# Softcapped attention: inverse norms are spread, and sums of squares turned, by transposes where products with the identity did it

## The chip, the core and the metric

The kernel runs on one core of a Trainium2 chip. A core has five engines that work side by side and wait for each other by semaphores: TensorE (PE in the profile, its weight loads PEld), VectorE (DVE), ScalarE (ACT), GpSimd (POOL) and SyncE (SP), which issues DMAs. TensorE reads a stationary operand (the weight load) and a moving one from SBUF and writes to PSUM, which has eight banks of 512 float32 a partition. The metric is the time on the device in microseconds, the lower the better.

## The reference

The program is a chain of sixteen layers on 1024 tokens of width 256 (mixers and feed-forward layers in turn), all in float32 but for a few bfloat16 parts. The change touches one layer, an attention of 16 heads of width 128 with normed queries and keys and a soft cap on its scores:

```python
q, k, v = x @ wq.T, x @ wk.T, x @ wv.T          # 16 heads of 128
q = rmsnorm(q, q_norm_w)                        # x * rsqrt(mean(x * x) + 1e-6) * w
k = rmsnorm(k, k_norm_w)
q, k = apply_rope(q, cos, sin), apply_rope(k, cos, sin)
scores = einsum('bhtd,bhsd->bhts', q, k) * 128 ** -0.5
scores = 50.0 * tanh(scores / 50.0)
...                                             # causal mask, softmax, times v, times wo
```

## The kernel before

`capped_attention` works on one head at a time, and makes the next head's operands while it works on this one. q and k lie with the width of the head (128) on the partitions and the 1024 tokens along the row, in two halves of 512. The rotation and the norms' weights enter as one factor for each row (`pair`). What is left of the two norms is one number for each token: the inverse root of its mean square.

The steps of a head, all in the order of one list that TensorE, VectorE and GpSimd follow:

```python
STEPS = "s0 s1 q0 s2 k0 o0 s3 q1 o1 s4 k1 o2 s5 o3 s6 m0 v0 s7 t0 v1 s8 s9 s10 b0 s11 b1 o4 o5 o6 o7".split()
```

The steps s and o belong to this head, the others make the next one. s0 to s3 are the scores of the first 512 queries with key tiles 0 to 3, s4 to s11 those of the second 512 with key tiles 0 to 7 (line 1602; narrower beyond the diagonal, so s8 has 512 columns, s9 384, s10 256, s11 128). ScalarE takes the tanh of each (line 1654) and the exponential of the unit before it (line 1661), in the order tanh 8, exponential 7, tanh 9, exponential 8. GpSimd multiplies the 128 columns on the diagonal by the causal mask (line 1519); for s8 that is mask 4. o0 to o7 (line 1611) are the outputs of the eight query tiles, over t + 1 key tiles each; output t waits for mask t and for a free bank of two. VectorE divides by the sum.

Of the makes, q, k and v are products with the weights (lines 1584 and 1593), copied by VectorE. GpSimd squares q and k. Step m (line 1558) sums the squares over the partitions, by four products with ones that leave each sum on 32 equal rows of a quarter of the bank: 128 rows of 512. VectorE makes means of them (line 1698). Step t (line 1567) turns these, so that tokens lie on the partitions: four products whose stationary operand is a 128x128 piece of `means` and whose moving operand is every 32nd column of the identity, four columns. VectorE copies the 16 columns (line 1703), and GpSimd raises them to the power -0.5 (line 1511): `inverse`, with columns 0 to 7 for the queries and 8 to 15 for the keys. The keys' norm is applied as the scale of the tanh. The queries' must be spread over all rows: step b (line 1590), twice four products with one column of `inverse`, broadcast to 128x128, as the stationary operand and the identity as the moving one. VectorE multiplies q by the result (line 1720), which ends the making of a head; the first score of the next head waits for it.

Head 0 is made ahead of all scores, in the order q0 k0 q1 k1 v0 m0 t0 v1 b0 b1; there ScalarE and VectorE make the inverse root. The last head has no makes beside it.

Of the kernel before, what the change touches and what calls it, by code (L numbers as in the profile page):

```python
# [13 lines left out]
P = 128  # L14
TOK = 1024
D = 256
NT = TOK // P
# [1404 lines left out]
QUARTER = P // 4  # L1422


def capped_attention(core, name, w, turns, heads, softcap):
# [5 lines left out]
    nc, x, hT = core.nc, core.x, core.hT  # L1431
    scale = P ** -0.5 / softcap
    NU = len(UNITS)
    with ExitStack() as layer:
        rows = layer.enter_context(nc.sbuf_tensor(f"{name}_rows", [P, NT, heads * P], F32))
        wo = layer.enter_context(nc.sbuf_tensor(f"{name}_wo", [P, heads, D], F32))
        with Stage(core, name) as st:
# [5 lines left out]
            means = st.sb("means", [P, HALF])  # L1443
# [3 lines left out]
            inverse = [st.sb(f"inverse{n}", [P, 2 * NT]) for n in range(2)]  # L1447
# [10 lines left out]
            ps_out, ps_sums = [core.bank(pairs[2] + n) for n in range(2)], core.bank(pairs[1] + 1)  # L1458
# [24 lines left out]
            @block.sync  # L1483
            def _(sp):
                for h in range(2, heads):
                    sp.wait_ge(made, (h - 1) * NM - 2)
                    sp.dma_start(w[h % 2][:], core.dram[f"{name}_w"][h]).then_inc(w_in[h % 2], 16)
                sp.dma_start(wo[:], core.dram[f"{name}_wo"]).then_inc(wo_in, 16)
                sp.wait_ge(wo_in, 16)
# [56 lines left out]
            @block.tensor  # L1546
            def _(pe):
                pe.sem_inc(summed, TILES)

                def make(h, e, step):  # L1550

                    kind, half = step[0], int(step[1])
                    if kind == "m":
                        if h == 0:
                            pe.wait_ge(filled, 9)
                        pe.wait_ge(squared, h * 4 + 4)
                        for n in range(4):
                            last = nc.tensor.matmul(ps_sums[n * QUARTER:(n + 1) * QUARTER, :],
                                                    core.ones[:, 0:QUARTER],
                                                    squares[:, n // 2, n % 2 * HALF:(n % 2 + 1) * HALF],  # L1560
                                                    start=True, stop=True)
                        last.then_inc(squares_summed, 1)
                        return
                    if kind == "t":
                        pe.wait_ge(meaned, h + 1)
                        for i in range(4):
                            last = nc.tensor.matmul(ps_sums[:, 4 * i:4 * i + 4], means[:, i * P:(i + 1) * P],
                                                    core.ident[:, ::QUARTER], start=True, stop=True)
                        last.then_inc(means_turned, 1)
                        return  # L1570
                    n = made_order.index(step)
                    if h == 0 and (n, 0) in begun:
                        pe.sem_inc(made, 1)
                        return
                    if h or n >= 4:
                        pe.wait_ge(kept, h * NM + (n - 2 + 1 + TWO))
                    to = make_bank(h, n)
                    if step == "q0" and h >= 2:
                        pe.wait_ge(w_in[e], 16 * (h // 2))
                    if kind == "b":  # L1580
                        pe.wait_ge(inverted, h + 1)
                    for c in range(DC if kind in "qk" else 0):
                        at = "qk".index(kind) * P
                        last = nc.tensor.matmul(to[:], w[e][:, c, at:at + P], hT[:, c, half * HALF:(half + 1) * HALF],  # L1584
                                                start=(c == 0), stop=(c == DC - 1))
                    for i in range(4 if kind in "vb" else 0):
                        t = 4 * half + i
                        part = to[:, i * P:(i + 1) * P]
                        if kind == "b":
                            last = nc.tensor.matmul(part, inverse[e][:, t:t + 1].broadcast_to([P, P]), core.ident[:],  # L1590
                                                    start=True, stop=True)
                        for c in range(DC if kind == "v" else 0):
                            last = nc.tensor.matmul(part, hT[:, c, t * P:(t + 1) * P], w[e][:, c, 2 * P:],
                                                    start=(c == 0), stop=(c == DC - 1))
                    last.then_inc(made, 1)

                def score(h, e, u):
                    kt, half, at = span(u)
                    if u == 0:
                        pe.wait_ge(kept, h * NM + (NM + TWO))  # L1600
                    pe.wait_ge(capped, h * NU + (u - 3 + 1 + THREE))
                    nc.tensor.matmul(ps_scores[u % 3][:, at:], k[e][:, kt * P:(kt + 1) * P],  # L1602
                                     q[e][:, half * HALF + at:(half + 1) * HALF], start=True, stop=True
                                     ).then_inc(scored, 1)

                def output(h, e, t):
                    pe.wait_ge(masked, h * NT + (t + 1))
                    pe.wait_ge(scaled, h * NT + (t - 2 + 1 + TWO))
                    at = t % 4 * P
                    for kt in range(t + 1):  # L1610
                        last = nc.tensor.matmul(ps_out[t % 2][:, 0:P + 1],  # L1611
                                                weights[UNITS.index((kt, t // 4))][:, at:at + P], v[e][:, kt, :],
                                                start=(kt == 0), stop=(kt == t))
                    last.then_inc(summed, 1)

                def head(h, e, more):
                    for step in STEPS:
                        if step[0] == "s":
                            score(h, e, int(step[1:]))
                        elif step[0] == "o":  # L1620
                            output(h, e, int(step[1:]))
                        elif more:
                            make(h + 1, 1 - e, step)

                for step in FIRST_MAKES:
                    make(0, 0, step)
                for g in range(0, heads // 2 - 1):
                    head(2 * g, 0, True)
                    head(2 * g + 1, 1, True)
                head(heads - 2, 0, True)  # L1630
                head(heads - 1, 1, False)
# [44 lines left out]
            def _(dve):  # L1676
# [16 lines left out]
                def keep_made(h, e, step):  # L1693
                    kind, half = step[0], int(step[1])
                    if kind == "m":

                        dve.wait_ge(squares_summed, h + 1)
                        nc.vector.tensor_scalar(means[:], ps_sums[:], factors[:, 0:1], factors[:, 1:2],
                                                ALU.mult, ALU.add).then_inc(meaned, 1)
                        return  # L1700
                    if kind == "t":
                        dve.wait_ge(means_turned, h + 1)
                        nc.vector.tensor_copy(turned[:].rearrange("p (n i) -> p n i", n=4),
                                              ps_sums[:, 0:2 * NT].rearrange("p (i n) -> p n i", n=4)
                                              ).then_inc(turned_kept, 1)
                        return
                    n = made_order.index(step)
                    src = make_bank(h, n)
                    part = slice(half * HALF, (half + 1) * HALF)
                    dve.wait_ge(made, h * NM + (n + 1))  # L1710
                    if kind == "q":
                        nc.vector.tensor_copy(q[e][:, part], src[:]).then_inc(kept, 1)
                    elif kind == "k":
                        nc.vector.tensor_copy(k[e][:, part], src[:]).then_inc(kept, 1)
                    elif kind == "v":
                        nc.vector.tensor_copy(v[e][:, 4 * half:4 * half + 4, 0:P],
                                              src[:].rearrange("p (t c) -> p t c", t=4)).then_inc(kept, 1)
                    else:
                        dve.wait_ge(kept, h * NM + (3 + TWO))
                        nc.vector.scalar_tensor_tensor(q[e][:, part], q[e][:, part], pair[:, 0, bass.ds(h, 1)], src[:],  # L1720
                                                       ALU.mult, ALU.mult).then_inc(kept, 1)
# [1950 lines left out]
```

## Time and profile before

| | us |
|---|---|
| three runs | 3126.07, 3129.86, 3134.58 |
| their median | 3129.86 |
| the profiled execution | 3134.99 |
| its span on the core | 3133.3 |
| granted clock of TensorE, mean share | 0.985 |

| engine, over the span | busy us | share |
|---|---|---|
| TensorE, products | 2929.5 | 93% |
| TensorE, weight loads | 1767.0 | 56% |
| VectorE | 1386.0 | 44% |
| ScalarE | 1104.9 | 35% |
| GpSimd | 560.3 | 18% |

Busy shares are means over sixteen layers with different limits, so the rows below are those of the layer's own stretch. A record is one instruction as the profiler sees it; a record of TensorE lasts longer than the distance to the next one's start, since they are pipelined. The pace is read from starts.

### The profile page before, as it was taken

The page shows a single profiled execution, that of the slowest core. Times are in us where ns is not written, and L with a number is a line of the kernel's source. Part 1 is how long each engine was busy: PE and PEld are TensorE (multiplying, and loading weights), DVE is VectorE, ACT ScalarE, POOL GpSimd, SP SyncE. Part 2 cuts the span into 40 slices and gives each one's busy share as a digit, 9 for nine tenths or more (in the row PEclk, how much of TensorE's full clock was granted, in tenths as well). Part 3 has the DMA queues.
Part 4 walks back from the last instruction along what each step waited for, and adds up shares of the span by engine and source line. Part 5 has one row for each costly group of instructions (what it writes and reads, how often), then busy time and mean ns, then how long its engine had stood idle before and what let it go on. Part 6 is the DMA issues. An engine that isn't in the chain of part 4 may idle for free. (4 is left out here: it accounts for less than half of the span.)

```text
span 3133.3 us, 39636 instructions
## 1 busy us (share of the span) xinstructions
PE 2929.5 (93%) x14853; PEld 1767.0 (56%) x14853; DVE 1386.0 (44%) x3153; ACT 1104.9 (35%) x1979; POOL 560.3 (18%) x686
## 2 busy tenths in 40 slices
PE   7989999889999999999999999999999999989756
PEld 3453455644465556556666666656776778644413
DVE  6758425576144114212233333434333332277597
ACT  3645514446132113111433433323333333246432
POOL 2020001130002222222000000013333331130163
PEclk9999999999989999999999999999999999999999
DMA  3021000020102231322100000000000000120131
GB/s 95 18 62 48 25 24 27 9 75 2 49 12 84 82 101 46 94 83 83 43 11 11 11 16 22 1 31 11 16 16 11 16 33 13 37 71 14 55 132 61
DMA packets 70505, 129.23 MB, mean 41 GB/s; under 512 B 15918, under 2 KB 43920, under 8 KB 70048
## 3 DMA queue, kind: packets, MB, share of 16 engines
q1 hardware_dynamic: 68396, 125.12, 13.4%
q10 hardware_dynamic: 1920, 1.57, 0.3%
q8 instruction: 120, 1.97, 0.3%
q14 instruction: 69, 0.57, 0.1%
HBM read 99.55 MB, written 1.54 MB: 32 GB/s over the span
## 5 line engine op out<-in xcount | busy, mean ns | idle before, releaser
L222 POOL TENSOR_TENSOR scale<-scale,powers 128x1 f32<-128x1 f32 (+1 forms) x98 | 57.4, 586 | 1461.3 <-DVE scale L203 1461.3
L2450 DVE TENSOR_TENSOR L1f_inner<-psum,L1f_gate 128x512 f32<-128x512 f32 x96 | 66.3, 691 | 352.7 <-PE psum L2347 352.5
L1654 ACT ACTIVATE L2b_tanh<-psum,L2b_inverse 128x512 f32<-128x512 f32 x192 | 110.6, 580 | 285.5 <-PE psum L1602 285.5
L2431 ACT ACTIVATE L1f_gate<-psum 128x512 f32<-128x512 f32 x96 | 57.2, 597 | 389.8 <-PE psum L2325 389.7
L1229 ACT ACTIVATE L0f_weights<-psum 128x1024 f32<-128x1024 f32 (+1 forms) x192 | 148.9, 812 | 111.3 <-PE psum L1053 84.5
L2304 POOL TENSOR_TENSOR L1f_inner<-L1f_inner,L1f_weight 128x512 f32<-128x512 f32 x96 | 119.2, 1265 | 358.3 <-DMA L1f_weight<-combine 343.0
L1611 PEld LDWEIGHTS psum<-L2b_v,L2b_weights 128*128 128x128 f32 x1152 | 141.3, 193 | 33.7 <-issue 28.7
L2091 ACT ACTIVATE L2a_probs<-psum,L2a_negmax 128x512 f32<-128x512 f32 (+7 forms) x128 | 95.0, 742 | 172.3 <-DVE L2a_negmax L2125 172.2
L1602 PE MATMUL psum<-L2b_q,L2b_k 128*128 128x512 f32 (+3 forms) x384 | 147.4, 487 | 1.0 <-DVE L2b_q L1720 0.8
L1611 PE MATMUL psum<-L2b_v,L2b_weights 128*128 128x129 f32 x1152 | 143.7, 277 | 2.9 <-POOL L2b_weights L1519 2.8
L1978 PE MATMUL psum<-L2a_k,L2a_q 128*128 128x512 f32 (+3 forms) x384 | 145.1, 487 | 0.0
L2125 DVE TENSOR_REDUCE L2a_negmax<-psum 128x1 f32<-128x512 f32 (+7 forms) x128 | 96.5, 755 | 81.6 <-PE psum L1980 81.5
L2135 DVE COPY L2a_probsT<-psum 128x512 f32<-128x512 f32 (+1 forms) x64 | 31.4, 491 | 228.3 <-PE psum L1991 228.3
L3077 PE MATMUL psum<-scan_seen,ident 128*128 128x512 f32 x128 | 65.7, 638 | 70.3 <-DVE scan_seen L3037 70.3
L2009 PE MATMUL psum<-L2a_probsT,L2a_v 128*128 128x512 f32 (+3 forms) x384 | 130.8, 490 | 0.3 <-DVEq L2163 0.3
L1020 PE MATMUL psum<-L0f_ks,L0f_qs 96*128 96x512 bf16 (+3 forms) x384 | 109.6, 333 | 17.9 <-DVE L0f_piece_max L1313 11.3
L2352 PE MATMUL psum<-L1f_w,L1f_inner 128*128 128x256 f32 x512 | 122.9, 379 | 0.0
L1961 PE MATMUL psum<-hT,L2a_early 128*128 128x512 f32 x248 | 119.8, 606 | 0.7 <-PEq L102 0.7
L2347 PE MATMUL psum<-hT,L1f_w 128*128 128x512 f32 x256 | 120.3, 592 | 0.0
L2325 PE MATMUL psum<-hT,L1f_w 128*128 128x512 f32 x256 | 120.3, 592 | 0.0
L1313 DVE TENSOR_REDUCE L0f_piece_max<-psum 128x1 f32<-128x512 f32 (+2 forms) x176 | 110.2, 682 | 22.3 <-PE psum L1020 13.0
L1584 PE MATMUL psum<-hT,L2b_early 128*128 128x512 f32 x248 | 116.5, 593 | 0.9 <-PEq L102 0.9
(520 smaller groups left out, 6091.4 us busy)
## 6 DMA issues: line engine op xcount, KB each, us to landing
L1f_w<-in_L1f_w SPq DMA_DIRECT2D x32, 384.0 KB, 3.6
L1f_weight<-combine SPq DMA_DIRECT2D x32, 384.0 KB, 4.4
L1f_weight<-combine SPq DMA_DIRECT2D x32, 256.0 KB, 4.6
scan_spread_b<-bc SPq DMA_DIRECT2D x16, 512.0 KB, 4.4
scan_spread_c<-bc SPq DMA_DIRECT2D x16, 512.0 KB, 4.0
L0f_qs<-L0f_part SPq DMA_DIRECT2D x96, 64.0 KB, 2.6
experts_early<-in_L1f_w SPq DMA_DIRECT2D x16, 384.0 KB, 3.4
L2a_early<-in_L2a_w SPq DMA_DIRECT2D x16, 384.0 KB, 3.0
```

The lines of the kernel that those rows point to most:

```text
L1229: nc.scalar.activation(weights[g % BUFFERS][:, :, at:], ps_scores[g % 2][:, :, at:], ACT.Exp, scale=HD ** -0.5).then_inc(exped, 1)
L1584: last = nc.tensor.matmul(to[:], w[e][:, c, at:at + P], hT[:, c, half * HALF:(half + 1) * HALF], start=(c == 0), stop=(c == DC - 1))
L1602: nc.tensor.matmul(ps_scores[u % 3][:, at:], k[e][:, kt * P:(kt + 1) * P], q[e][:, half * HALF + at:(half + 1) * HALF], start=True, stop=T ...
L1611: last = nc.tensor.matmul(ps_out[t % 2][:, 0:P + 1], weights[UNITS.index((kt, t // 4))][:, at:at + P], v[e][:, kt, :], start=(kt == 0), st ...
L1654: nc.scalar.activation(tanhs[u % 3][:, at:], ps_scores[u % 3][:, at:], ACT.Tanh, scale=inverse[e][:, NT + kt:NT + kt + 1]).then_inc(capped, 1)
L1961: last = nc.tensor.matmul(to[:], w[h % 2][:, c, at:at + P], hT[:, c, half * HALF:(half + 1) * HALF], start=(c == 0), stop=(c == DC - 1))
L1978: nc.tensor.matmul(ps_scores[i % 2][:, a:b], q[h % 2][:, t * P:(t + 1) * P], k[h % 2][:, a:b], start=True, stop=b < width(i))
L2009: last = nc.tensor.matmul(to[:, at:], v[h % 2][:, kt, :], probsT[h % 2][half][:, kt, at:], start=(kt == 0), stop=(kt == tiles - 1))
L2304: nc.gpsimd.tensor_tensor(inner[u % INNER][:], inner[u % INNER][:], weight[n % SPREAD][:, half * HALF:(half + 1) * HALF], ALU.mult).then_i ...
L2325: last = nc.tensor.matmul(ps_gate[u % 2][:], w[n % RING][:, c * P:(c + 1) * P], hT[:, c, tokens_of(u)], start=(c == 0), stop=(c == DC - 1 ...
L2347: last = nc.tensor.matmul(ps_up[u % 2][:], w[n % RING][:, D + c * P:D + (c + 1) * P], hT[:, c, tokens_of(u)], start=(c == 0), stop=(c == D ...
L2352: return nc.tensor.matmul(out_of(t), inner[u % INNER][:, t % 4 * P:(t % 4 + 1) * P], w[u // 2 % RING][:, 2 * D:3 * D], start=(u == 0), sto ...
```

## The change

In step t the four products become four transposes, whose moving operand is the whole identity: each writes 128 columns of the bank where four were written, and the columns that the kernel needs lie 32 apart in it. The copy behind it picks them. In step b the eight products of a head become eight transposes of the same broadcast operand. Every engine issues as many instructions as before, in the same order.

```diff
                     if kind == "t":
                         pe.wait_ge(meaned, h + 1)
                         for i in range(4):
-                            last = nc.tensor.matmul(ps_sums[:, 4 * i:4 * i + 4], means[:, i * P:(i + 1) * P],
-                                                    core.ident[:, ::QUARTER], start=True, stop=True)
+                            last = nc.tensor.transpose(ps_sums[:, i * P:(i + 1) * P], means[:, i * P:(i + 1) * P],
+                                                       core.ident[:])
...
                         part = to[:, i * P:(i + 1) * P]
                         if kind == "b":
-                            last = nc.tensor.matmul(part, inverse[e][:, t:t + 1].broadcast_to([P, P]), core.ident[:],
-                                                    start=True, stop=True)
+                            last = nc.tensor.transpose(part, inverse[e][:, t:t + 1].broadcast_to([P, P]), core.ident[:])
...
                     if kind == "t":
                         dve.wait_ge(means_turned, h + 1)
                         nc.vector.tensor_copy(turned[:].rearrange("p (n i) -> p n i", n=4),
-                                              ps_sums[:, 0:2 * NT].rearrange("p (i n) -> p n i", n=4)
+                                              ps_sums[:].rearrange("p (i n r) -> p n i r", n=4, r=QUARTER)[:, :, :, 0]
                                               ).then_inc(turned_kept, 1)
```

## Rows read from the trace of the kernel before

**Rows 1.** Windows, all engines; columns in its first line.

```profile
core 0: us, PE busy (x) PEld busy (x) DVE busy (x) ACT busy (x) POOL busy (x), PEclk, DMA share, GB/s
2140.00:2600.00 460.00, 457.81 (x2668) 328.40 (x2666) 160.87 (x398) 176.99 (x369) 159.78 (x199) 1.00 0.05 17
```

**Rows 2.** Groups by line; columns: line, engine, operation, names, shapes, count, busy us, mean ns, idle.

```profile
L1590 PE MATMUL psum<-ident,L2b_inverse 128*128 128x128 f32 x256 | 33.8, 275 | 0.0
...
L1797 PE MATMUL psum<-ident,L2b_rows 128*128 128x128 f32 x128 | 18.9, 273 | 1.0 <-PEq L102 1.0
...
L1567 PE MATMUL psum<-ident,L2b_means 128*128 128x4 f32 x128 | 15.3, 243 | 0.9 <-DVE L2b_means L1698 0.9
```

**Rows 3.** Timeline of 2309.2 to 2310.8; columns: start us, us, engine, line, names, count, idle.

```profile
2309.49 0.86 PEld L1567 LDWEIGHTS psum<-ident,L2b_means 128*128 128x128 f32 x7 [0.24 <-issue]
...
2310.27 0.64 PEld L1593 LDWEIGHTS psum<-L2b_early,hT 128*128 128x128 f32 x5
...
2310.47 0.17 DVE L1703 COPY L2b_turned<-psum 128x16 f32<-128x16 f32 x1 [0.96 <-PE psum L1567]
2310.73 2.90 POOL L1511 TENSOR_TENSOR L2b_inverse<-L2b_turned,L2b_power 128x16 f32<-128x16 f32 x1 [6.35 <-DVE L2b_turned L1703]
```

**Rows 4.** Timeline of TensorE, stage behind this one.

```profile
2619.07 0.60 PE L1797 MATMUL psum<-ident,L2b_rows 128*128 128x128 f32 x4
2619.51 1.89 PE L1806 MATMUL psum<-L2b_wo,L2bo_turned 128*128 128x256 f32 x8
```

**Rows 5.** Timeline of 2312.5 to 2317.4, all engines.

```profile
2312.16 2.10 PE L1602 MATMUL psum<-L2b_q,L2b_k 128*128 128x512 f32 x6
...
2313.22 0.69 ACT L1654 ACTIVATE L2b_tanh<-psum,L2b_inverse 128x512 f32<-128x512 f32 x1 [2.33 <-PE psum L1602]
...
2313.89 1.08 PEld L1590 LDWEIGHTS psum<-ident,L2b_inverse 128*128 128x128 f32 x8
2314.10 1.05 PE L1590 MATMUL psum<-ident,L2b_inverse 128*128 128x128 f32 x8
...
2314.79 0.63 ACT L1661 ACTIVATE L2b_weights<-L2b_tanh 128x512 f32<-128x512 f32 x1
...
2315.21 1.06 PE L1590 MATMUL psum<-ident,L2b_inverse 128*128 128x128 f32 x8
...
2315.49 0.46 POOL L1519 TENSOR_TENSOR L2b_weights<-L2b_weights,L2b_keep 128x128 f32<-128x128 f32 x1 [1.87 <-ACT L2b_weights L1661]
...
2316.01 1.53 PEld L1611 LDWEIGHTS psum<-L2b_v,L2b_weights 128*128 128x128 f32 x13
...
2316.11 1.51 PE L1611 MATMUL psum<-L2b_v,L2b_weights 128*128 128x129 f32 x12
```

**Rows 6.** Timeline of GpSimd, one head earlier.

```profile
2280.62 2.90 POOL L1511 TENSOR_TENSOR L2b_inverse<-L2b_turned,L2b_power 128x16 f32<-128x16 f32 x1 [6.35 <-DVE L2b_turned L1703]
2285.39 0.46 POOL L1519 TENSOR_TENSOR L2b_weights<-L2b_weights,L2b_keep 128x128 f32<-128x128 f32 x1 [1.87 <-ACT L2b_weights L1661]
```

**Rows 7.** Timeline of TensorE, then of VectorE, in head 0.

```profile
2138.24 2.10 PE L1590 MATMUL psum<-ident,L2b_inverse 128*128 128x128 f32 x16
2141.18 0.70 PE L1602 MATMUL psum<-L2b_q,L2b_k 128*128 128x512 f32 x1 [0.84 <-DVE L2b_q L1720]
...
2138.44 0.69 DVE L1716 COPY L2b_v<-psum 128x512 f32<-128x512 f32 x1 [1.18 <-PE psum L1593]
...
2140.38 0.75 DVE L1720 SCALAR_TENSOR_TENSOR L2b_q<-L2b_q,L2b_pair,psum 128x512 f32<-128x512 f32 x1 [0.30 <-PE psum L1590]
```

**Rows 8.** Timeline of TensorE and windows (of line 1611, then of all engines).

```profile
2607.13 7.71 PE L1611 MATMUL psum<-L2b_v,L2b_weights 128*128 128x129 f32 x52 [1.55 <-POOL L2b_weights L1519]
...
3014.93 1.98 PE L3077 MATMUL psum<-scan_seen,ident 128*128 128x512 f32 x4 [1.70 <-DVE scan_seen L3037]
...
2608.10:2611.50 3.40, 3.40 (x18) 3.40 (x17) 0.50 0.00 0
2611.50:2614.90 3.40, 3.34 (x30) 3.15 (x29) 1.00 0.00 0
...
2990.50:3100.00 109.50, 59.03 (x120) 20.09 (x119) 104.66 (x61) 32.43 (x29) 65.80 (x28) 1.00 0.36 119
```

## The prediction

> **What bounds the kernel now.** I read the windows table first, for the stage of the change, the softcapped attention. Between 2140 and 2600 us TensorE is busy for 457.81 of 460.00 us at a granted clock of 1.00 (2.4 GHz), VectorE, ScalarE and GpSimd for about 35 to 38% each [rows 1]. So TensorE's order of work sets the time, and an instruction less on TensorE is worth its time only if what stands behind it is ready. Second came the groups by line, for how many records one call leaves. A float32 product leaves two records: line 1590 runs 16 heads x 8 = 128 calls and has 256, line 1567 runs 64 calls and has 128. A float32 transpose leaves one: line 1797 has 8 tiles x 16 chunks = 128 calls and 128 records [rows 2]. Third, the timeline at the two places of the change, with all engines, for what arrives just in time.
>
> **Step t, the turning of the sums (line 1567).** In the head at 2309 us seven weight loads start between 2309.49 and 2310.27, where the next step's loads begin: 0.78 / 7 = 0.111 us each [rows 3]. They set the pace, since four columns take less; eight make 0.89 us a head. Line 1797 shows four transposes of 128x128 float32 between 2619.07 and 2619.51: 0.44 us, 0.11 each [rows 4]. The saving is 0.89 - 0.44 = 0.45 us a head. That every transpose now writes 128 columns costs nothing more: 0.11 is the price of 128 columns.
>
> What follows t: the copy on VectorE (2310.47, 0.17 us), then the power on GpSimd (2310.73, 2.90 us), ready at 2313.63 [rows 3]; the first load of line 1590, which waits for it, is at 2313.89 [rows 5]. That leaves 0.26 us. The copy now takes 16 elements out of 512 columns, at a step of 32 elements where it was 4 and less. No row shows this shape; it may be no dearer than 0.17 us or take the 0.69 us that a copy of all 512 columns takes [rows 7], which would use up the 0.26 and stop TensorE for 0.3 us. I take 0.17, since the same count of elements is read; the dear end costs nothing either, because of the wait below, which holds later work by more than that. Work between the end of t and this load (step v1, scores 8 to 10) is not changed, and the last record of t ends about as long before v1 as it did. So t's 0.45 us moves everything behind it forward: 16 x 0.45 = 7.2 us. The price is bounded by no gain (if a transpose of this tile still took two records, as line 1590 does) and by 0.89 us a head (if it were free), 0 to 14 us.
>
> The Trainium skill has another price for this: "TensorE: Matmul & The Clock Gate", section Terms, says that the transpose mode is four times faster for FP32. By that rule four transposes would take 0.22 us and the saving of t would be 0.67 us a head, 10.7 us in all. The rows on line 1797 show half of a product, not a quarter, so I take half.
>
> **Step b, the spreading of the inverse norms (line 1590).** Four products take from 2315.21 to 2316.11 = 0.90 us, the other four of the head (2314.10) as long; eight transposes would take 8 x 0.11 = 0.88 instead of 1.79, which is 0.91 us less work on TensorE a head, 14.6 us in 16 heads [rows 4, 5]. But look at what stands behind. The order there is score 8, 9, 10, b0, score 11, b1, output 4. Output 4 (line 1611) waits for GpSimd's mask of the weights that come from score 8. That chain does not pass through b: score 8 on TensorE starts at 2312.16, its tanh on ScalarE at 2313.22 (ScalarE had idled 2.33 us for it), then the exponential of unit 7, the tanh of unit 9, the exponential of unit 8 at 2314.79, then the mask at 2315.49 for 0.46 us, ending at 2315.95. The weight load of output 4 stands at 2316.01, 0.06 us after, and its first product at 2316.11 [rows 5]. TensorE shows no idle time there, as it has just finished b1; so the page's waits hardly show this wait. Both chains now arrive within a few hundredths of each other: 3.95 us from the start of score 8 to output 4, both by TensorE's own work and by way of ScalarE and GpSimd. One head earlier the mask stands at 2285.39, which is 30.10 us before 2315.49, just as the two powers stand 30.11 apart [rows 3, 6]: it repeats to the hundredth.
>
> So when b gets shorter by 0.91 us, output 4 still starts 3.95 us after score 8, and TensorE idles for 0.91 us ahead of it. ScalarE's four activations and the mask are untouched and start no earlier, as they wait for score 8. Gain of b in heads 1 to 15 (made while the head before is worked on): 0 as I take it, the end at 0.91 us each standing as the rival below. Nothing behind is hurt: outputs 5 to 7 wait for masks that keep their distance to mask 4, and VectorE's queue has room.
>
> Head 0 is different: its b is made before any score, and the path is TensorE, VectorE, TensorE. Now: b from 2138.24, the second scaling of q at 2140.38 for 0.75 us, the first score at 2141.18 [rows 7]. Then: the fourth transpose starts at 2138.24 + 3 x 0.11 and is through 0.27 us later (the mean of one record [rows 2]), at 2138.84, but VectorE's copy of v, from 2138.44, lasts 0.69 us to 2139.13; two scalings of 0.75 with 0.04 us between end at 2140.71, and the score starts about 2140.76, 0.42 us earlier. The end without a gain is 0; a gain over 0.91 us is excluded by TensorE's own work. I take 0.4.
>
> **Sum.** 7.2 (t) + 0 (b, heads 1 to 15) + 0.4 (b, head 0) = 7.6 us. The profiled execution took 3134.99 us (span 3133.3); so 3127.4 for such an execution. The median of the runs shown is 5.1 us lower, 3129.86: 3129.9 - 7.6 = 3122.3 us, 0.24% less.
>
> **Rivals.**
>
> Full gain: the wait ahead of output 4 gives way with b, or the chain over ScalarE has slack that the rows don't show. Then b brings 15 x 0.91 = 13.7 us more: 3108.6 us. For it speaks that no idle time stands on TensorE there in the trace; against it the mask that ends 0.06 us ahead of the load it releases. Chance 0.15.
>
> Cheaper transposes, by the rule quoted above: 10.7 + 0.4 = 11.1 us, 3118.8 us. Against it stand all 128 records of line 1797. Chance 0.02.
>
> No gain: the transposes do not do what the change says in this form, because the stationary side is a column broadcast by a zero step or because 128 columns go out where 4 did, and each takes two records or their time. Then 3129.9 us. For it: no transpose in the trace reads a broadcast operand. Against it: that operand is read today at the pace of any product, 0.11 us a record [rows 5], and t has no such operand. If it touches b alone, nothing changes in the forecast but 0.4 us. Chance 0.10.
>
> Slower: the clock. TensorE would then idle 0.91 us ahead of output 4 in each head, just behind 0.9 us of transposes. Behind a gap of 1.55 us at 2607.13 the granted clock stood at 0.50 (1.2 GHz) from 2608.1 to 2611.5, and only 18 records of line 1611 fit there against 30 in the next 3.4 us [rows 8]. That costs 12 x 0.11 = 1.3 us each time. Once a head it is 15 x 1.3 = 20 us, and the time 3122.3 + 20 = 3142 us. It decides from the point where the clock falls in more than 6 of the 15 heads (7.6 / 1.3), all at output 4. Against it: in the scan TensorE idles 1.70 us ahead of every four products, and from 2990.5 to 3100 the clock stays at 1.00 with TensorE busy for 59.03 of 109.50 us [rows 8]. Chance 0.07.
> The Trainium skill gives this rival its reason: "TensorE: Matmul & The Clock Gate", Part 4, says that a transpose does not count as work for the clock gate as a product does. By that rule the quiet stretch would be some 1.8 us long instead of 0.9. No row isolates it.
>
> **How the numbers follow.** The forecast has 0.66, full gain 0.15, cheaper transposes 0.02, no gain 0.10, the clock 0.07. A measurement of this kernel can tell about 0.3% (9.4 us) from no change; the three runs of before alone lie between 3126.07 and 3134.58. The forecast of 0.24% falls under that bound, but near it: with an error of some 3 us in a median about 0.26 of its chance lies over it, 0.17. So faster: 0.15 + 0.02 + 0.17 = 0.34. Same: 0.49 + 0.10 = 0.59 less 0.01 for a slow tail = 0.58. Slower: 0.07 + 0.01 = 0.08. The range leaves out the clock and nearly all of the full gain, and holds the rest with 3 to 4 us of spread: 3111 to 3130 us. The forecast's own range is 3118 to 3127.
>
> **What the changed profile would show.** Line 1567 with 64 records of 128 columns, line 1590 (then the transpose) with 128, each step of four taking 0.44 us. One head lasting 29.65 us where it lasts 30.10. An idle time of about 0.9 us on TensorE ahead of output 4, released by GpSimd's mask, 15 times, about 13.5 us together, and still 3.95 us from the start of score 8 to the first product of output 4. If that idle time is missing and a head lasts 28.7 us, my reading of the mask is wrong. If a head lasts 29.65 us but idle time stands ahead of the first transpose of b0, the copy on VectorE has become dear. If the granted clock shows 0.50 inside the stage, the last rival holds.

## The result, and the profile after

Each kernel ran twenty times. One run of the changed kernel took 6002.38 us; it is left out of the ratio as slow, and no profile of it shows why. The median of the changed kernel's other nineteen is 3120.35 us (3120.77 with it), that of the kernel before is 3130.03. The ratio, which is estimated from the runs and is not that of the two medians, is 0.9964, with a 95% interval from 0.9949 to 0.9978: 11.3 us less (6.9 to 16.0), where the medians are 9.7 us apart. The same changed kernel, timed again beside the experiments, came to 0.9975 (0.9956 to 0.9993). The forecast was 7.6 us less, a ratio of 0.9976.

The page of the changed kernel, its span and its busy times:

```profile
span 3118.3 us, 39239 instructions
...
PE 2902.9 (93%) x14648; PEld 1741.5 (56%) x14661; DVE 1384.1 (44%) x3153; ACT 1104.8 (35%) x1979; POOL 560.3 (18%) x686
```

The span is 15.0 us shorter (3133.3 before), and the layer of the change holds only part of that. TensorE's first product of the layer starts at 2122.05, and at 2128.07 in the profile before: 6.0 us lie ahead of any changed instruction. They go with the clock: up to there the granted clock stood at 0.50 for 61.4 us in the profile before and for 47.8 us in this one. Here are the layer's first row in the profile before, then that of the stage behind:

```profile
2128.07 3.67 PE L1584 MATMUL psum<-hT,L2b_early 128*128 128x512 f32 x8 [0.86 <-PEq L102]
```

```profile
2615.83 1.50 PE L1797 MATMUL psum<-ident,L2b_rows 128*128 128x128 f32 x12 [0.99 <-PEq L102]
```

And after, TensorE at the start with the making of head 0, VectorE there, then TensorE at the end:

```profile
2122.05 3.67 PE L1584 MATMUL psum<-hT,L2b_early 128*128 128x512 f32 x8 [0.87 <-PEq L102]
...
2131.71 0.60 PE L1590 MATMUL psum<-ident,L2b_inverse 128*128 128x128 f32 x4
2132.66 0.65 PE L1590 MATMUL psum<-ident,L2b_inverse 128*128 128x128 f32 x4 [0.35 <-DVE L2b_v L1715]
2134.15 1.77 PE L1601 MATMUL psum<-L2b_q,L2b_k 128*128 128x512 f32 x4 [0.84 <-DVE L2b_q L1719]
```

```profile
2131.92 0.69 DVE L1715 COPY L2b_v<-psum 128x512 f32<-128x512 f32 x1 [1.08 <-PE psum L1592]
2132.53 1.57 DVE L1719 SCALAR_TENSOR_TENSOR L2b_q<-L2b_q,L2b_pair,psum 128x512 f32<-128x512 f32 x2
```

```profile
2593.25 6.07 PE L1610 MATMUL psum<-L2b_v,L2b_weights 128*128 128x129 f32 x52 [1.55 <-POOL L2b_weights L1519]
2600.31 1.50 PE L1796 MATMUL psum<-ident,L2b_rows 128*128 128x128 f32 x12 [0.99 <-PEq L102]
```

From the first product to the first transpose of the stage behind, the layer took 2615.83 - 2128.07 = 487.76 us, and takes 2600.31 - 2122.05 = 478.26: 9.50 less. Of these, 1.64 us is the low clock that the profile before has over the last outputs [rows 8]: there the 52 products to the next stage span 2615.83 - 2607.13 = 8.70 us, here 7.06. The rest is the change's own, 7.86 us.

The groups by line and the windows answer to [rows 1, 2]:

```profile
L1590 PE MATMUL psum<-ident,L2b_inverse 128*128 128x128 f32 x128 | 19.3, 273 | 0.3 <-DVE L2b_v L1715 0.3
...
L1567 PE MATMUL psum<-ident,L2b_means 128*128 128x128 f32 x64 | 9.7, 273 | 0.9 <-DVE L2b_means L1697 0.9
```

```profile
2140.00:2580.00 440.00, 430.35 (x2448) 300.73 (x2447) 156.41 (x389) 170.26 (x355) 156.54 (x193) 1.00 0.05 17
```

Every transpose is one record: 128 where there were 256 on line 1590, 64 where there were 128 on line 1567. TensorE is busy for 430.35 us of the window's 440.00, where it was for 439.16 of the same window before, at the same clock of 1.00.

The timeline of step t, which answers to [rows 3]:

```profile
2300.17 0.60 PE L1567 MATMUL psum<-ident,L2b_means 128*128 128x128 f32 x4
...
2300.61 1.17 PE L1592 MATMUL psum<-L2b_early,hT 128*128 128x128 f32 x9
2300.81 0.17 DVE L1702 COPY L2b_turned<-psum 128x16 f32<-128x16 f32 x1 [0.61 <-PE psum L1567]
...
2301.06 2.90 POOL L1511 TENSOR_TENSOR L2b_inverse<-L2b_turned,L2b_power 128x16 f32<-128x16 f32 x1 [6.00 <-DVE L2b_turned L1702]
```

Four transposes take 2300.61 - 2300.17 = 0.44 us. The copy out of 512 columns takes 0.17 us, as the one out of 16 did, and the power starts 0.25 us behind the start of the copy (0.26 before).

The timeline from score 8 to output 4, which answers to [rows 5]:

```profile
2302.39 2.10 PE L1601 MATMUL psum<-L2b_q,L2b_k 128*128 128x512 f32 x6
...
2303.45 0.69 ACT L1653 ACTIVATE L2b_tanh<-psum,L2b_inverse 128x512 f32<-128x512 f32 x1 [1.88 <-PE psum L1601]
...
2304.11 0.57 PEld L1590 LDWEIGHTS psum<-ident,L2b_inverse 128*128 128x128 f32 x4
2304.33 0.60 PE L1590 MATMUL psum<-ident,L2b_inverse 128*128 128x128 f32 x4
...
2304.99 0.60 PE L1590 MATMUL psum<-ident,L2b_inverse 128*128 128x128 f32 x4
2305.02 0.63 ACT L1660 ACTIVATE L2b_weights<-L2b_tanh 128x512 f32<-128x512 f32 x1
...
2305.72 0.45 POOL L1519 TENSOR_TENSOR L2b_weights<-L2b_weights,L2b_keep 128x128 f32<-128x128 f32 x1 [1.77 <-ACT L2b_weights L1660]
...
2306.23 0.85 PEld L1610 LDWEIGHTS psum<-L2b_v,L2b_weights 128*128 128x128 f32 x7 [0.89 <-POOL L2b_weights L1519]
2306.23 0.94 PE L1610 MATMUL psum<-L2b_v,L2b_weights 128*128 128x129 f32 x6 [0.64 <-POOL L2b_weights L1519]
```

b0 and b1 take 0.44 us each. Then TensorE waits: the bracket on output 4 names GpSimd's mask, with 0.64 us from the end of the last transpose's record. Counted by starts the wait is longer: the next product could have started at 2304.99 + 0.44 = 2305.43, and starts at 2306.23, 0.80 us later. The mask ends at 2306.17, its load follows at 2306.23. Before, the load came at 2316.01 behind a mask that ended at 2315.95. In both, 3.33 us pass from the start of score 8 to that of the mask (2302.39 to 2305.72, and 2312.16 to 2315.49). GpSimd's queue one head earlier answers to [rows 6]:

```profile
2271.41 2.90 POOL L1511 TENSOR_TENSOR L2b_inverse<-L2b_turned,L2b_power 128x16 f32<-128x16 f32 x1 [6.00 <-DVE L2b_turned L1702]
2276.07 0.46 POOL L1519 TENSOR_TENSOR L2b_weights<-L2b_weights,L2b_keep 128x128 f32<-128x128 f32 x1 [1.76 <-ACT L2b_weights L1660]
```

The powers stand 2301.06 - 2271.41 = 29.65 us apart, and 30.11 before.

### The profile page after: what moved, and what is told of

Read it like the earlier page. It is cut to its first block and busy times, and to the rows that moved or that the text cites. A ratio compares the mean times of both kernels' runs of the same rounds, so it can differ in the third digit from the quotient of the medians.

```text
span 3118.3 us, 39239 instructions
## 1 busy us (share of the span) xinstructions
PE 2902.9 (93%) x14648; PEld 1741.5 (56%) x14661; DVE 1384.1 (44%) x3153; ACT 1104.8 (35%) x1979; POOL 560.3 (18%) x686
## 3 DMA queue, kind: packets, MB, share of 16 engines
q10 hardware_dynamic: 1920, 1.57, 0.3%
HBM read 99.55 MB, written 1.54 MB: 32 GB/s over the span
```

## The experiments

They were timed beside the kernel before, in two sessions on two chips: the first four rows below it with 12 runs each beside 35 of the kernel before, the last three with 10, 6 and 12 beside 21. "A head" is the distance of GpSimd's powers (line 1511), as a mean over 12 heads. "Layer" is the time from its first product to the first transpose behind it.

| kernel | ratio (95%) | a head, us | head 0, first product to first score | layer |
|---|---|---|---|---|
| before | 1 | 30.105 | 13.11 | 487.76, 1.64 of it low clock |
| changed, again | 0.9975 (0.9956 to 0.9993) | 29.648 | 12.11 | 478.26 |
| t alone | 0.9980 (0.9961 to 0.9999) | 29.650 | 12.61 | 478.80 |
| b alone | 0.9987 (0.9968 to 1.0005) | 30.104 | 12.61 | 485.59 |
| score 8 ahead of v1 | 0.9948 (0.9930 to 0.9965) | 29.199 | 12.10 | 471.51 |
| exponential 7 first | 0.9953 (0.9935 to 0.9971) | 29.198 | 12.10 | 471.50 |
| scores 8 and 9 ahead | 0.9935 (0.9912 to 0.9958) | 28.739 | 12.10 | 464.62 |
| the same order, products | 0.9998 (0.9981 to 1.0015) | 30.104 | 13.11 | 486.10 |

**The changed kernel again.**

> The changed kernel unaltered, beside the others on one chip. Theory (the wait for mask 4 hides step b): 7.9 us below the kernel before inside the layer (15 heads x 0.457 us, and 1.0 us in head 0), so a ratio near 0.9975; a low-clock stretch of TensorE more or less is 1.4 us each. Rival (the change brings more than its layer's trace shows): a ratio of 0.9964 or less, as first measured, 11 us or more, and a head below 29.6 us.

The head, head 0 and the layer repeat the first profile to 0.01 us. The layer's 7.9 us make a ratio of 0.9975, and that is what was measured. The rival (0.9964 or less, and a shorter head) did not come.

**One step alone.** In the first kernel step b is products again, in the second step t is.

```diff
 t alone, against the changed kernel
-                            last = nc.tensor.transpose(part, inverse[e][:, t:t + 1].broadcast_to([P, P]), core.ident[:])
+                            last = nc.tensor.matmul(part, inverse[e][:, t:t + 1].broadcast_to([P, P]), core.ident[:],
+                                                    start=True, stop=True)
 b alone, against the kernel before
-                            last = nc.tensor.matmul(part, inverse[e][:, t:t + 1].broadcast_to([P, P]), core.ident[:],
-                                                    start=True, stop=True)
+                            last = nc.tensor.transpose(part, inverse[e][:, t:t + 1].broadcast_to([P, P]), core.ident[:])
```

> Only step t is a transpose; step b is products as before. Theory: one head lasts 29.65 us, as in the changed kernel, no idle time ahead of output 4, 15 x 0.457 + 0.45 = 7.3 us below the kernel before. Rival (b counts on TensorE's path in every head): it misses b's part, so 29.65 us a head can't be reached and the gain is some 3 us.

> Only step b is transposes; step t is four products of four columns. Theory: one head lasts 30.10 us as before, 0.8 us of TensorE's time ahead of output 4 go idle in each of 15 heads, and only head 0 gains: 0.4 to 0.6 us in all, ratio 0.9998. Rival (b's time comes back): 15 x 0.91 = 13.7 us less, a head of 29.2 us.

With t alone a head is as short as with both, and TensorE has work up to output 4; the timeline, from b1 on:

```profile
2211.85 1.06 PE L1590 MATMUL psum<-ident,L2b_inverse 128*128 128x128 f32 x8
...
2212.13 0.45 POOL L1519 TENSOR_TENSOR L2b_weights<-L2b_weights,L2b_keep 128x128 f32<-128x128 f32 x1 [1.76 <-ACT L2b_weights L1661]
...
2212.64 0.75 PEld L1611 LDWEIGHTS psum<-L2b_v,L2b_weights 128*128 128x128 f32 x6
...
2212.74 0.72 PE L1611 MATMUL psum<-L2b_v,L2b_weights 128*128 128x129 f32 x5
```

With b alone a head is as long as before the change, and b's time stands as a wait for the mask, 0.65 us by the row's bracket:

```profile
2216.30 0.46 POOL L1519 TENSOR_TENSOR L2b_weights<-L2b_weights,L2b_keep 128x128 f32<-128x128 f32 x1 [1.87 <-ACT L2b_weights L1660]
...
2216.81 0.71 PE L1610 MATMUL psum<-L2b_v,L2b_weights 128*128 128x129 f32 x4 [0.65 <-POOL L2b_weights L1519]
```

So in heads 1 to 15 all of the gain is t's, and b's work there is hidden. In head 0 each step brings 0.50 us. In the layer t alone brings 7.3 us (486.12 - 478.80, the first being the 487.76 of before less its 1.64 of low clock) and b alone 0.5. The ratios alone could not have told this: their intervals overlap, and it is the head's length in the profiles that does.

**Score 8 earlier.** The edit is in the list of steps of the changed kernel:

```diff
-STEPS = "... s7 t0 v1 s8 s9 s10 b0 s11 b1 o4 o5 o6 o7".split()
+STEPS = "... s7 t0 s8 v1 s9 s10 b0 s11 b1 o4 o5 o6 o7".split()
```

> The changed kernel with score 8 put ahead of step v1 in the list of steps (s7 t0 s8 v1 s9 s10 b0 s11 b1), so that 1.8 us more of TensorE's work lie between score 8 and output 4: 4.8 us against the 3.84 that the chain by ScalarE and GpSimd takes. Theory: the idle time ahead of output 4 goes, a head lasts 28.8 us, 15 x 0.81 = 12 us below the changed kernel, 20 us below the kernel before (ratio 0.9936). Rival (another wait takes its place, the power on GpSimd ahead of mask 4 or ahead of b0 above all): most of the 12 us stay away.

It gained about half of what I expected: a head of 29.20 us, not 28.8. The timeline from the tanh of unit 9 on:

```profile
2211.45 0.58 ACT L1653 ACTIVATE L2b_tanh<-psum,L2b_inverse 128x384 f32<-128x384 f32 x1 [1.23 <-PE psum L1601]
...
2211.93 0.62 ACT L1660 ACTIVATE L2b_weights<-L2b_tanh 128x512 f32<-128x512 f32 x1
...
2212.62 0.46 POOL L1519 TENSOR_TENSOR L2b_weights<-L2b_weights,L2b_keep 128x128 f32<-128x128 f32 x1 [1.31 <-ACT L2b_weights L1660]
...
2213.14 1.05 PE L1610 MATMUL psum<-L2b_v,L2b_weights 128*128 128x129 f32 x7 [0.20 <-POOL L2b_weights L1519]
```

ScalarE idles 1.23 us for score 9, which is still behind v1, and takes exponential 8, for which all was ready, only after. The wait of TensorE is shorter (0.20 us in the row), and it is still the mask's. GpSimd's power, my rival, had ended at 2211.31, 1.3 us ahead of the mask.

**Exponential 7 first.** The changed kernel, with another order on ScalarE alone:

```diff
+                        if u == 8:
+                            weigh(h, 7)
                         if u < NU:
                             cap(h, e, u)
-                        if u >= 1:
+                        if u >= 1 and u != 8:
                             weigh(h, u - 1)
```

> The changed kernel; ScalarE takes the exponential of unit 7 ahead of the tanh of unit 8, in time in which it idles for score 8. Theory (output 4 waits by way of ScalarE): the chain from the start of score 8 to output 4 becomes tanh 8, tanh 9 (which then waits for score 9, 0.06 us), exponential 8, mask: 3.37 us instead of 3.84. TensorE's own work there takes 3.04 us, so 0.33 us of idle time stay; a head lasts 29.18 us, 7 us below the changed kernel, ratio near 0.9952. Rival (the wait is for something else than this chain): a head of 29.65 us as in the changed kernel, ratio 0.9975.

```profile
2211.22 1.23 ACT L1653 ACTIVATE L2b_tanh<-psum,L2b_inverse 128x512 f32<-128x512 f32 x2 [1.36 <-PE psum L1601]
...
2212.35 0.62 ACT L1660 ACTIVATE L2b_weights<-L2b_tanh 128x512 f32<-128x512 f32 x1
...
2213.04 0.45 POOL L1519 TENSOR_TENSOR L2b_weights<-L2b_weights,L2b_keep 128x128 f32<-128x128 f32 x1 [1.31 <-ACT L2b_weights L1660]
...
2213.55 0.38 PE L1610 MATMUL psum<-L2b_v,L2b_weights 128*128 128x129 f32 x1 [0.19 <-POOL L2b_weights L1519]
```

A head lasts 29.20 us where 29.18 was expected. No instruction of TensorE was touched: that 0.45 us a head came from moving one activation into idle time of ScalarE shows that output 4 waited by way of ScalarE.

**Scores 8 and 9 earlier**, in the changed kernel and in the kernel before:

```diff
-STEPS = "... s7 t0 v1 s8 s9 s10 b0 s11 b1 o4 o5 o6 o7".split()
+STEPS = "... s7 t0 s8 s9 v1 s10 b0 s11 b1 o4 o5 o6 o7".split()
```

> The changed kernel with scores 8 and 9 ahead of step v1 (s7 t0 s8 s9 v1 s10 b0 s11 b1). In the run with score 8 alone ahead, a head lasted 29.20 us, since ScalarE took tanh 9 ahead of exponential 8 and waited for score 9 behind v1. Theory: with score 9 ahead as well the chain to output 4 is 3.84 us again beside 4.8 us of TensorE's work, no idle time is left, a head lasts 28.84 us, 20 us below the kernel before, ratio 0.9936. Rival (GpSimd's power of 2.9 us, which is ahead of mask 4 in its queue, becomes the wait): a head stays over 29.1 us.

> The kernel before the change, products in t and b, with scores 8 and 9 ahead of step v1. Theory (before the change TensorE's work sets the time and the mask is just in time): the order gives nothing, a head lasts 30.10 us less some 0.01, ratio 1.0000. Rival (the order alone brings the gain): a head below 29.9 us and a ratio below 0.997.

With the transposes:

```profile
2211.36 0.57 ACT L1653 ACTIVATE L2b_tanh<-psum,L2b_inverse 128x384 f32<-128x384 f32 x1
2211.82 0.63 ACT L1660 ACTIVATE L2b_weights<-L2b_tanh 128x512 f32<-128x512 f32 x1
...
2212.53 0.46 POOL L1519 TENSOR_TENSOR L2b_weights<-L2b_weights,L2b_keep 128x128 f32<-128x128 f32 x1
...
2213.91 1.53 PEld L1610 LDWEIGHTS psum<-L2b_v,L2b_weights 128*128 128x128 f32 x13
2214.01 1.50 PE L1610 MATMUL psum<-L2b_v,L2b_weights 128*128 128x129 f32 x12
```

The mask ends at 2212.99, 0.92 us before the load that waits for it, and no bracket of a wait is left. A head lasts 28.74 us: 0.91 less than in the changed kernel, which is all of b's saving. The median was 3107.95 us (six runs) against 3127.95 before, a ratio of 0.9935 (0.9912 to 0.9958). That it is also faster than the changed kernel rests on the profiles, where its layer is 13.6 us shorter (15 x 0.909); the two were not timed in one session, and their intervals touch.

With products the same order gives nothing:

```profile
2219.47 0.46 POOL L1519 TENSOR_TENSOR L2b_weights<-L2b_weights,L2b_keep 128x128 f32<-128x128 f32 x1 [1.10 <-ACT L2b_weights L1661]
...
2220.21 0.53 PEld L1611 LDWEIGHTS psum<-L2b_v,L2b_weights 128*128 128x128 f32 x4
2220.32 0.50 PE L1611 MATMUL psum<-L2b_v,L2b_weights 128*128 128x129 f32 x3
```

The mask has 0.28 us to spare here, and TensorE is full, so a head stays 30.104. With products in t and b the order is worth nothing, and with the order as it was b is worth nothing in these heads. The shorter b pays once the other chain is started earlier or shortened, as exponential 7 ahead of tanh 8 did for half of it. This kernel also has the end of the layer at full clock, which shows what the low clock in the profile before cost:

```profile
2601.64 6.07 PE L1611 MATMUL psum<-L2b_v,L2b_weights 128*128 128x129 f32 x52 [1.55 <-POOL L2b_weights L1519]
2608.70 1.50 PE L1797 MATMUL psum<-ident,L2b_rows 128*128 128x128 f32 x12 [0.98 <-PEq L102]
```

2608.70 - 2601.64 = 7.06 us against 8.70 [rows 8].

## Why the prediction was right

Step t: 0.45 us a head forecast, 30.105 - 29.648 = 0.457 measured, and the kernel with t alone shows it by itself. The half price of a transpose held (0.44 us for four, where four products took 0.89), so the rival with a quarter of the price, 0.22 us, fell. The copy at a step of 32 elements, bounded between 0.17 and 0.69 us, took 0.17.

Step b in heads 1 to 15: 0 forecast, 0.001 us a head measured with b alone. The wait for mask 4 came where it was placed, with the 3.33 us chain unchanged. The loss of 0.91 us was right, but no row of a product shows it whole: it is 0.80 us between starts of products and 0.11 us by which the first product's record now starts too early, together with its weight load (last section). So the time from score 8 to the first product is 3.84 us (2306.23 - 2302.39), where the prediction had 3.95 stay.

Step b in head 0: 0.4 us forecast, 0.50 measured. The prediction had the first scaling start 0.04 us behind the end of the copy of v; it starts at 2132.53, 0.08 us before that end (2131.92 + 0.69 = 2132.61). That is 0.12 us sooner, of which the two scalings give 0.03 back (1.57 us, where the prediction had 1.54). The prediction left out one wait: between the two spreads TensorE waits 0.35 us for the copy of v, whose bank it needs. That wait is not free. The second spread ends at 2132.66 + 0.65 = 2133.31, and the second scaling starts only at 2133.35, 0.09 us after the first has ended, so here VectorE waits for TensorE. In a later head, where both spreads are done in time, the two scalings span 1.41 us:

```profile
2304.97 1.41 DVE L1719 SCALAR_TENSOR_TENSOR L2b_q<-L2b_q,L2b_pair,psum 128x512 f32<-128x512 f32 x2 [1.68 <-PE psum L1590]
```

By these two rows I estimate that the wait for the bank costs head 0 up to 0.16 us.

The sum: 7.6 us forecast, 7.86 measured in the layer. The first comparison's 11.3 us lies above both, and its interval (6.9 to 16.0) holds them, as does that of the second (2.2 to 13.8). The range of the prediction, 3111 to 3130 us, is wide enough to hold no gain as well, so it is the length of a head and the place of the wait that bear the forecast out, more than the time.

Two things in the traces and runs say that what exceeds 7.9 us is the clock of single executions and not the change. First, the layer starts at 2128.1 us in the profile before, and between 2116.9 and 2122.6 in the eight others, two of which have products in t. If half of the time that the clock had stood at 0.50 by then (37.6 to 61.4 us) is taken off, all nine starts lie between 2096.1 and 2098.2. Second, among the runs of one kernel the time falls as the mean granted clock rises, by 2.6 to 2.9 us for each 0.001. A line through each kernel's runs, read at a clock of 0.987, gives 3120.4 us for the first nineteen of the changed kernel and 3120.5 for the twelve later ones, against 3128.1 for the 35 of the kernel before in the same session as these (3127.5 in the other session): 7.6 to 7.8 us less, or 7.0 to 7.1. The clocks of the first twenty runs of the kernel before were not kept, so the first ratio itself can't be corrected this way.

The rivals. Full gain fell by the kernel with b alone. No gain fell by the counts of records, also for the broadcast operand. The slower clock fell: in the changed kernel's two profiles, and in the six of the experiments, the granted clock was 1.00 all through the layer, though the changed kernel has a wait of 0.8 us behind 0.9 us of transposes in each head. The one low stretch in the layer, in the profile of the kernel before, cost 1.64 us, where this rival had put 1.3. By the rule of Part 4 of "TensorE: Matmul & The Clock Gate" in the Trainium skill, that a transpose does not count as busy time of TensorE in the same way, a low clock could have come here; none did. Twelve transposes in 29.65 us of products are little to try that rule on.

## What to carry to other kernels

An engine that is 99% busy hides the waits that would begin if its work got shorter. Before pricing a saving there, look at each semaphore wait behind it and at when it was released: a release 0.06 us ahead of its use meant here that the saving was worth nothing in that place. Where two chains arrive together, both must get shorter. Here an order that starts the other chain earlier cost nothing while TensorE was full (a head of 30.104 us against 30.105), and paid 0.91 us a head as soon as it was not.

## What the runs showed of the hardware

A wait ahead of a weight load is longer than the brackets on the products say. In a full queue a load starts 0.11 us ahead of its product. In the changed kernel output 4's first load and first product both start at 2306.23: the record of the product starts with its load. It lasts 0.38 us in the row that holds it alone, against 0.28 in a full queue, and the second product follows 0.215 us behind it instead of 0.11. From the first load to the second product it is 0.216 us in both kernels, so the load is where to count from. Without the wait it would have started with the last transpose (2304.99 + 3 x 0.11 = 2305.32), as it does in the kernel with scores 8 and 9 ahead; it starts 0.91 us later. That kernel got back just this: 29.648 - 28.739 = 0.909 us a head. The brackets of the changed kernel's rows say 0.64 for the product and 0.89 for the load.

The weight load of a float32 transpose is also shorter, 0.137 us on line 1590 where that of a product took 0.190, with the same broadcast operand of zero step. The pace hardly changed with it: transposes start 0.109 us apart, the records of products 0.111, whether their moving operand had 128 columns (line 1590) or four (line 1567). What of load and columns sets that pace, these runs do not separate.
